# Another order for the same instructions: new due times for the list that a planner writes (four batches of two attention and feed-forward layers, one core)

## The reference, cut to what matters

```python
x = x + attn_a(layernorm(x))   # 16 heads of 16, causal softmax over 1024 keys, with biases
x = x + ffn(layernorm(x))      # silu(x Wg) * (x Wu), hidden width 768, then Wd
x = x + attn_b(layernorm(x))   # 16 heads of 16, each query sees the last 64 keys
x = x + ffn(layernorm(x))      # the same weights again
```

## Time and profile before

| what | value |
|---|---|
| median of 3 runs | 1201.09 us (1200.05 to 1207.57) |
| the profiled execution | 1202.65 us |
| its span, first to last instruction | 1200.9 us |
| mean granted clock of TensorE | 0.985 |
| TensorE (PE) busy | 1096.6 us, 91% |
| VectorE (DVE) busy | 810.4 us, 67% |
| ScalarE (ACT) busy | 739.7 us, 62% |
| GpSimd (POOL) busy | 381.3 us, 32% |

### The profile page before, as it was taken

How to read it: one execution, slowest core, us unless ns; L and a number is a source line. 1 busy time by engine, 2 the same in 40 slices (tenths; PEclk the granted TensorE clock), 3 DMA queues, 4 the chain that set the end, 5 groups by cost and what they waited for, 6 DMA issues and landing times.

```text
span 1200.9 us, 32268 instructions
## 1 busy us (share of the span) xinstructions
PE 1096.6 (91%) x13309; PEld 668.1 (56%) x13309; DVE 810.4 (67%) x1546; ACT 739.7 (62%) x1060; POOL 381.3 (32%) x385
## 2 busy tenths in 40 slices
PE   7878898999998889999999889999899898999997
PEld 5433247766773326766775234776686332477666
DVE  6798826756878853666797792675588778166552
ACT  5366783665556785476555778466646577746653
POOL 7632142123234314202324413222223332421242
PEclk9899999999999999999999999999999899999999
DMA  8610001041132000122223000103023100011201
GB/s 300 213 61 16 7 11 52 32 132 61 51 108 65 16 7 26 60 65 83 81 73 108 21 8 11 52 31 131 28 70 100 49 17 11 7 51 50 63 20 37
DMA packets 70385, 71.64 MB, mean 60 GB/s; under 512 B 26016, under 2 KB 62304, under 8 KB 69344
## 3 DMA queue, kind: packets, MB, share of 16 engines
q1 hardware_dynamic: 70240, 69.56, 17.6%
HBM read 23.60 MB, written 8.39 MB: 27 GB/s over the span
## 4 chain that ended last, share of the span: by engine, by line
PE 65%; DVE 16%; ACT 7%; issue 5%; DMA 3%; POOL 3%; SPq 0%; POOLq 0%; ACTq 0%; DVEq 0%
PE ring L1715 11%; PE ring L1747 8%; PE ring L1748 7%; PE ring L1682 6%; DVE peak L1269 5%; PE ring L1637 5%; ACT probs_causal L1470 4%; PE ring L1761 4%; PE ring L1766 3%; DVE peak_c L1269 3%; PE ring L1587 3%; DVE xn L1162 2%; PE ring L1589 2%; PE ring L1588 2%; PE ring L1607 2%
## 5 line engine op out<-in xcount | busy, mean ns | idle before, releaser
L1470 ACT ACTIVATE probs_causal<-ring 128x1024 f32<-128x1024 f32 (+1 forms) x320 | 286.2, 941 | 130.8 <-PE ring L1682 76.8
L1269 DVE TENSOR_REDUCE peak<-ring 128x2 f32<-128x1024 f32 (+5 forms) x320 | 323.3, 1031 | 55.8 <-PE ring L1637 32.9
L1682 PE MATMUL ring<-q_st,k_st 64*64 64x192 f16 (+5 forms) x2752 | 168.1, 296 | 29.6 <-ACT probs_causal L1470 17.4
L1137 POOL TENSOR_TENSOR h_lo<-h_f,h_hi 128x512 fp32r<-128x512 f32 x96 | 122.1, 1289 | 181.8 <-ACT h_hi L1504 181.5
L1715 PE MATMUL ring<-probs_causal,V 128*32 128x512 f32 (+3 forms) x1536 | 165.8, 513 | 6.1 <-POOL probs_causal L1122 4.6
L1747 PE MATMUL ring<-xf_hi,w_gu_sb 128*128 128x512 f32 x384 | 159.3, 415 | 4.4 <-DVE xf_lo L1169 3.1
L1128 POOL TENSOR_TENSOR onf<-osb,onf 128x512 f32<-128x512 f32 x64 | 81.7, 1277 | 237.4 <-DVE onf L1312 236.9
L1122 POOL TENSOR_SCALAR_AFFINE_SELECT probs_causal<-probs_causal 128x512 f32<-128x512 f32 x128 | 80.7, 634 | 226.2 <-ACT probs_causal L1470 225.8
L1748 PE MATMUL ring<-xf_lo,w_gu_sb 128*128 128x512 f32 x384 | 151.6, 395 | 0.0
L1682 PEld LDWEIGHTS ring<-q_st,k_st 64*64 64x64 f16 x2752 | 67.5, 106 | 144.6 <-ACT probs_causal L1470 68.8
L1637 PE MATMUL ring<-k_st,q_st 64*64 64x512 f16 (+7 forms) x1536 | 123.8, 340 | 25.3 <-DVE peak L1269 16.3
(11 more groups left out here) (157 smaller groups left out, 1974.3 us busy)
## 6 DMA issues: line engine op xcount, KB each, us to landing
q_st<-q_part SPq DMA_DIRECT2D x96, 128.0 KB
w_qkv<-img_qkv SPq DMA_DIRECT2D x7, 1536.0 KB, 7.6
on_lo<-onf SPq DMA_DIRECT2D x64, 128.0 KB, 2.6
k_st<-k_part SPq DMA_DIRECT2D x48, 144.0 KB, 2.1
k_st<-k_part SPq DMA_DIRECT2D x48, 128.0 KB, 2.1
y<-X SPq DMA_DIRECT2D x8, 512.0 KB, 3.0
wp_sb<-img_wp SPq DMA_DIRECT2D x7, 512.0 KB, 3.6
x_next<-in_x SPq DMA_DIRECT2D x3, 1024.0 KB, 5.4
```

Source lines behind the costliest of these rows:

```text
L1137: pool.tensor_tensor(h_lo[m][:], h_f[m][:], h_hi[m][:].bitcast(F32), ALU.subtract).then_inc(h_lo_done, 1)
L1269: dve.tensor_reduce(dst, scores, AX.X, ALU.max).then_inc(a_max, 1)
L1470: act.activation(in_banks(block[0:rows, n % slots], unit, w), heads_of(flat_of(a, e), unit, w)[0:rows], ACT.Exp, scale=back[a % 2]).then_i ...
L1682: last = pe.matmul(psum[BLOCK * m:BLOCK * m + BLOCK, r, per * n:per * n + w], keys[rows_of(r), head, first_key + BLOCK * m:first_key + BLO ...
```

## The change

Only the numbers of `LAYER_START` and `TIMES` change. The events, their steps, the costs in `steps`, the needs, the semaphores, the buffers, `SOON`, `TURN` and `RELOAD` stay. With other due times `order()` picks other steps where several are ready, and so the lists of the engines, the banks and the places and number of the filling matmuls come out differently. The core of the diff (the tables run on in the same manner for each kind):

```diff
-LAYER_START = (93.43, 161.02, 153.72, 527.89, 502.08, 575.15, 566.57, 604.82)
+LAYER_START = (28.36, 37.33, 43.45, 437.37, 441.58, 643.82, 729.37, 1036.47)
 TIMES = {
-    "Z": ((-511.27, 522.18, 624.41, -344.72, -834.4, -373.72, -330.28, -242), (-386.48, 318.23, 642.08, -223,
-        -833.33, -353.09, -286.94, 87.12)),
+    "Z": ((-826.35, 380.66, 849.79, -36.9, 783.27, 222.52, 874.87, 235.59), (-722.79, 505.92, 848.04, 283.37,
+        759.17, 378.94, 874.87, 358.56)),
...
-    "V": ((715.41, 795.52, 758.13, 702.17, 739.72, 772.83, 657.3, 796.72, 754.05, 711.27, 818.67, 754.3, 727.05,
+    "V": ((519.74, 526.6, 423.87, 460.15, 501.3, 510.85, 520.87, 457.78, 491.32, 516.08, 510.18, 522.58, 471.71,
...
-    "H": ((644.72, 648.8, 900, 900, -250.25, -223.57, -375.48, -370.4), (646.47, 621.41, 900, 900, -252.55,
-        -194.63, -377.34, -392.35)),
+    "H": ((765.07, 755.63, 76.69, 75.61, 863.25, 863.25, 117.9, 126.73), (709.8, 706.89, 74.29, 61.2, 863.25,
+        862.43, 123.7, 106.48)),
...
```

More of the change, by code:

```diff
@@ L68 @@
 I32 = mybir.dt.int32
-LAYER_START = (93.43, 161.02, 153.72, 527.89, 502.08, 575.15, 566.57, 604.82)
+LAYER_START = (28.36, 37.33, 43.45, 437.37, 441.58, 643.82, 729.37, 1036.47)
 TIMES = {
[104 rows of a table removed]
-    "Uqkv": ((-332.34,), (-422.11,), (-27.27,)),
-    "Uvalues": ((-498.15,), (-541.45,)),
-    "Ubq": ((-105.71,),),
-    "Ukpre": ((-107.66,),),
-    "Uatt_b": ((89.11,), (-50.07,), (113.91,)),
-    "Ub": ((-214.81,), (-111.07,), (-115.9,)),
-    "Uw": ((122.98, 7.46), (87.78, -36.12), (42.82, 30.69)),
-    "Ud": ((-78.84,), (-89.78,), (-57.09,)),
-    "Ug": ((219.51, -1.91), (220.93, 196.36), (187.11, 51.16)),
-    "Us": ((341.96, 518.07, 645.97),),
-    "Ut": ((302.6, 248.88, 216.79, 126.04),),
-    "Uc": ((156.38,), (196.26,), (233.62,), (180.87,)),
-    "Ux": ((-482.7, -143.66), (-470.6, -169.44), (-465.72, -151.15), (-384.64, -145), (-409.32, -105.32)),
-    "Up": ((-50.07, -95.88, -69.76, -142.67, -322.56, -329.09),),
-    "Fg": ((-201, -173.83, -160.95, -105.34),),
-    "x": ((598.12, 887.59),),
-    "Fw": ((-199.21, -243.47),),
-    "Fq": ((421.73, 437.83),),
-    "k": ((-100.06,),),
-    "Fs": ((-10.44, 270.84),),
-    "Fx": ((562.62,),),
-    "X": ((178.15, 105.38, 797.15, 781.29),),
[101 rows of a table added]
+    "Uqkv": ((-548.38,), (-548.36,), (-109.36,)),
+    "Uvalues": ((-695.19,), (-711.89,)),
+    "Ubq": ((-132.23,),),
+    "Ukpre": ((-99.8,),),
+    "Uatt_b": ((268.78,), (153.22,), (284.99,)),
+    "Ub": ((-205.55,), (-79.85,), (-102.4,)),
+    "Uw": ((127.92, -42.75), (147.93, -51.8), (99.49, 43.28)),
+    "Ud": ((-68.88,), (-26.55,), (-40.76,)),
+    "Ug": ((254.8, 2.63), (295.98, 96.08), (275.19, 18.81)),
+    "Us": ((431.64, 493.6, 846.05),),
+    "Ut": ((110.25, 136.97, 40.76, -35.88),),
+    "Uc": ((150.01,), (260.22,), (279.21,), (191.11,)),
+    "Ux": ((-629.22, -123.72), (-578.88, -74.3), (-591.22, -71.96), (-521.19, -74.91), (-521.57, -116.95)),
+    "Up": ((-24.86, -54.72, -79.39, -48.84, -321.02, -229.34),),
+    "Fg": ((-188.26, -129.35, -142.93, -182.67),),
+    "x": ((854.47, 885.57),),
+    "Fw": ((-277.01, -428.5),),
+    "Fq": ((217.83, 387.34),),
+    "k": ((887.55,),),
+    "Fs": ((-40.34, 224.26),),
+    "Fx": ((280.82,),),
+    "X": ((870.86, 869.83, 880.81, 880.81),),
 }
```

## The result

| | before | after |
|---|---|---|
| median of 16 runs each | 1202.21 us | 1208.86 us |
| lowest and highest | 1199.11, 1208.89 | 1203.61, 1216.86 |
| profiled execution, its span | 1202.65, 1200.9 | 1209.13, 1207.4 |
| granted clock in it | 0.985 | 0.979 |
| the planner's own total | 1170.47 | 1161.72 |

The ratio is 1.0053, with the interval 1.0032 to 1.0074: 6.65 us slower, half a per cent, inside the 1% that the prediction called no change, and on the other side of its forecast (the stated range, 1172 to 1214 us, reached over both signs). The planner had promised 8.75 us less. So there are 15.4 us to explain between what the plan says the new order does and what the chip says.

What follows compares the result with a forecast made beforehand. TensorE, busy 1096.6 of 1200.9 us, was taken to bound the kernel. Terms -15 (b), 0 (c), +2 (d), 0 (a, e) made -13 us, from the median 1201.1 to 1188 us; range 1172 to 1214.

Steps and rivals of the forecast that it cites:

- (b): Inside of the causal core: turned pairs bring back 0.4 of TensorE's idle time, 15 us gained; bounds 39 gained, 15 lost.
- (a): Big arrangement of layers and feed-forward blocks: same stretches with the same engines on top, 0 us.
- (c): End of the causal layer: two h_lo stay ahead of the last multiplication on GpSimd; 0 us, ends -5.4 and +5.4.
- (d): Hand-over from sliding to causal layer: roots part, two more table loads each; 2 us lost in all, ends 0 and 8.9.
- Rival 2: Hand-overs: late root of the sliding layer's feed-forward norm delays the next layer; slower, some 1216 us, chance 0.18.
- (e): Filling matmuls throughout the kernel follow the plan's gaps: 0 us, ends -2 and +2.
- Rival 1: Causal core bound by consumers' work, not turns: no measurable change, some 1197 us, chance 0.28.
- Rival 3: Causal core: nearly two thirds of its idle time come back; larger gain, some 1172 us, chance 0.12.

Runs made afterwards that it cites:

- e5: Changed kernel with the two steps splitting the maxima made reductions, second part left at zero: 1201.59 us, 0.9967 of the kernel before.
- e6: Kernel before with the two steps splitting the maxima made reductions, second part left at zero: 1201.35 us, ratio 0.9971.
- e13: e5 with the second and third hand-over from sliding to causal layer in the old order: 1196.62 us, 0.9931 of the kernel before.
- e3: Changed kernel, same order, with 230 filling matmuls in place of 178: 1209.95 us, 1.0036 of the kernel before.
- e4: Kernel before, same order, with 250 filling matmuls in place of 185: 1203.91 us, ratio 1.0004.
- e12: e5 with the second half of the first sliding layer and the first hand-over in the old order: 1197.48 us, 0.995 of the kernel before.
- e14: e5 with the three hand-overs and the three causal cores in the old order: 1198.38 us, 0.9952 of the kernel before.
- e10: e9 with two of each four useless matmuls as 64x64 tiles: 1312.88 us, 1.0897 of the kernel before.
- e9: Kernel before with four useless full-array matmuls ahead of each of 192 gate and up products: 1237.15 us, ratio 1.0274.
- e1: Changed kernel with the three hand-overs from sliding to causal layer in the old order: 1201.2 us, 0.9989 of the kernel before.

## Why the prediction was wrong

**What failed** is the premise of the sum, "every instruction keeps its duration, its DMAs and its waits". 144 instructions of 0.17 us don't: their duration depends on what GpSimd runs when they start, and the order decides that. Above 0.178 us each they took 4.2 us before and 17.9 after. The prediction had no term for it; from e5 and e6 it is worth 6.8 us between the orders, give or take 4.4, about as much as the measured +6.65. The second failure is the term of -15 us in (b), below. The trace of before showed it too: the maxima's splits had a longest of 894 and 1137 ns beside medians of 175 and 176, and the prediction went by the means of large groups only.

**(a)** held. The stretches stand in the same sequence with the same engines on top, 288 to 293 us apart (before 287 to 292), by the roots.

**(b)** failed in sign. The core of 70 us after, in the two batches that answer to the earlier trace rows:

```profile
367.00:437.00 70.00, 59.97 (x799) 21.09 (x797) 57.67 (x88) 49.01 (x60) 23.06 (x27) 0.93 0.11 35
...
655.00:725.00 70.00, 60.23 (x823) 23.35 (x827) 57.90 (x89) 51.27 (x64) 23.71 (x28) 0.98 0.11 35
```

TensorE idles for 10.0 and 9.8 us, not for 5 or 6 as forecast and not for 8.3 and 8.1 as before. Its weight loads wait for maxima for 12.0 and 12.4 us there, where it was 12.8 both times: nearly the same, the sign that the prediction itself gave for (b) being wrong. Only the first core gained: 77.24 us busy of 90, where there were 75.47. The 15 us rested on a share of the idle time between two ratios of waits, which no row priced. And the 14% of turned pairs is a count of due times: of the same 4496 pairs only 264, 6%, stand the other way round in the new list of TensorE. The plan itself had 8.75 us in all. What of that is real shows once the ports are out of it: at the full clock 0.6 to 0.7 us in a causal stretch (140.92 in e5; 141.51 and 141.66 in e6), and over the kernel 0 (e5 against e6). The mixture e13 (0.9931) lies 4.8 us under e6 (0.9971), at the edge of what the intervals tell.

**(c)** had the right sequence: two `h_lo` still stand ahead of the last multiplication. The chain of waits after:

```profile
178.01 2.49 POOL h_lo L1134 x2
180.50 1.25 POOL onf L1125
181.77 2.87 DMA on_lo<-onf
```

VectorE's spreading now ends at 177.51 and the multiplication starts at 180.50, so GpSimd's queue costs 2.99 us and not 1.35. In the other three batches it is 2.53, 2.95 and 2.94 after 1.30, 1.32 and 1.30: +6.1 us in four, just beyond the upper end of 5.4. It cost nothing that can be seen, as the causal tails (root at 421.02 to 476.69, at 428.49 to 484.20) take 55.7 us in both.

**(d)** failed. The table loads are 58 again, and both roots stand together behind the exponentials (ScalarE of the kernel after):

```profile
279.08 1.79 ACT L1467 ACTIVATE probs_sliding<-ring 128x768 f32<-128x768 f32 x3 [0.62 <-PE ring L1688]
280.89 1.28 ACT L1356 ACT_TABLE_LOAD   x1
282.18 0.20 ACT L1356 ACTIVATE table<-table 128x1 f32<-128x1 f32 x1
282.29 0.28 ACT L1345 ACTIVATE std<-mv 128x4 f32<-128x4 f32 x2
```

Here due times far apart did not part two steps, so the 2 us of (d) are 0. Rival 2 needed a late root. The kernel did get slower, but the stretch that should have grown, from the last sliding exponential to the first causal maximum, takes 23.1, 21.3 and 23.1 us where it took 22.7, 22.7 and 24.3: its direction came true by another cause. **(e)** fillers: 43.71 us for 44.89, as taken.

**Rival 1** forecast hardly any gain and was nearest, with the consumers' work as its reason; no run tests that reason. **Rival 3** found no room.

**What stays open.** Of the 15.4 us between plan and chip the ports account for 6.8, give or take 4.4. The mean clock over the runs is 0.0030 lower in the new order (0.9801; 0.9828 to 0.9835 in the kernel before, beside the experiments), which by the spread of the runs is 2.5 to 3 us; e5 still has it (0.9806) and e6 doesn't (0.9834), so it comes with the order and not with the ports. That is argued from a correlation, not shown: the one attempt to raise the clock (e3, e4) did not make the kernel faster. Some 6 us have no cause that the runs show, and the mixtures e12 to e14 are too close to each other to place them. Kernels with the true second part made by a form that needs no shared port were not tried.

## What to carry to other kernels

A list scheduler with fixed costs doesn't see that VectorE and GpSimd share ports. When an order changes, compare the busy time of each engine at equal counts, and where it moved look at the longest beside the median of its small instructions. A tiny step on the chain is best made a reduction, or given a form that reads PSUM; one input in SBUF is not enough, since the `tensor_scalar` of the split has only one and was held for up to 1.67 us. Moving it away from GpSimd in the plan recovers only part, because the chip's times are not the plan's. And 0.4% of a kernel like this is what one dip of the clock went with, so the verdict needs medians, and stretches are compared only at an equal clock.

## What the runs showed of the hardware

- A 128x16 VectorE step of 0.17 us took 1.67 and 2.28 us behind GpSimd additions of about 2.35 us, and 1.25 behind one of 1.27, each ending with the GpSimd instruction; 128 reductions of the same size in e5 stayed at or below 0.172 us. VectorE instructions that read PSUM beside SBUF kept their 0.68 and 0.74 us.
- A turn between the full array and 64x64 tiles cost 0.113 us, give or take 0.013 (670 of them, e10 less e9).
- Over the 16 runs of the new order time and mean granted clock go together (correlation -0.86), 8.3 us for each 0.01; in the runs beside e1, e5 and e9 the kernel before has 9.9, 8.6 and 10.0. In the 20 runs beside e12 it is 2.5 (correlation -0.27), so this is no fixed price. One causal stretch at 0.96 took 145.85 us for 141.2.
- More filling matmuls (52 and 65 more) raised the mean clock by about 0.005 and did not shorten either kernel measurably.
